# GpSimd waits, at every second group of four gathers, until all its gathers have landed

## The chip, the cores and the metric

The kernel runs on one core of a Trainium2 chip. The metric is the device time of one execution in microseconds (us). Most executions of this kernel lie within about 0.3% of each other.

## The reference, cut to what matters

`x` is 6250 x 256 in float32, with 200,000 edges `src`, `dst`, sorted by `dst`. One layer is computed:

```
xn = layernorm(x)
gnn:  h_neigh = xn @ W_neigh; keep the 32 largest of each row (h_sparse)
      summed[n] = sum over edges with dst == n of h_sparse[src];  neigh = summed / max(deg, 1)
      gnn = xn @ W_self + neigh
mix:  linear attention over all rows, a gelu/sigmoid gate, a projection
x   = x + gnn + mix
x   = x + ffn(layernorm(x))    # only the rows of the 3124 largest router weights get the ffn
```

What matters here is `summed`: for every edge a row of `h_sparse` must be fetched by its index `src` and added into the row `dst`.

## The kernel before, in words

Rows are cut into NT = 50 tiles of T = 125. A first pass (to about 275 us) computes `h_sparse` and writes it to the DRAM tensor `rows_d` as pairs of float16 (1 KB a row). Then the attention sums follow, and from about 365 us to 2216 us the main loop `positions`: ND = 5 blocks of PER = 10 positions, one position for one tile of destination rows.

Nine of ten positions in a block (s = 0 to 8) build their tile's sum from gathered rows. Edges are taken in chunks of 128, and GC = 4 chunks are a group. For each group GpSimd copies four columns of indices from `srcT` to `stage` (L573) and issues four indirect DMAs (L577), each of which fetches 128 rows of 1 KB from `rows_d` into one slot of `ring`. The ring has RING = 8 slots of a group. VectorE builds a one-hot matrix for each group (L1266), and TensorE multiplies it with the gathered rows (L916, four matmuls a group, in `visit`). The tenth position (s = 9) takes a dense tile instead: its edge counts are collected by windows in the nine positions before it (L1291 and L1293 on VectorE, L891 on TensorE), and the counts are multiplied with all of `rows_d`, which is read in three thirds into `hs` (L667, on ScalarE's DMA queue, 2.1 MB each). TensorE multiplies the thirds (L953) at s = 7, 8 and 9; `hs` holds one third, so thirds 1 and 2 are read only when the one before is used up.

The order of the gather work is set by semaphores:

- `s_land[c]`, one for each of the 32 chunks of the ring, is raised by 16 by each landed gather.
- SyncE (SP) runs a loop over all groups (L474 to L479): it waits for the four `s_land` of the group in order, and adds 1 to `s_landed`.
- TensorE waits in `visit` for `s_landed >= g + 1` (L910), and after the last matmul of a group adds 1 to `s_slot_free` (it starts at 8).
- GpSimd's queue for group g is: wait for `s_slot_free >= g + 2` (L569, that is, until group g - 7 is used up), copy the indices of group g + 1 to `stage` (L573), wait for the copy of group g's indices, issue the four gathers of group g. Groups are numbered g = 0, 1, 2, ... in what follows, q is g modulo 8.

`hold(engine, semaphore, value)` (L105) is a wait followed by a semaphore increment of a counter that nothing else waits for. GpSimd does nothing else in the main loop, and SP nothing but its counting loop.

Of the kernel before, what the change touches and what calls it, by code (L numbers as in the profile page):

```python
# [37 lines left out]
def build(nc, x_d, src_d, dst_d, w_self_d, w_neigh_d, wqkv_d, wproj_d, bproj_d, ln_g_d, ln_b_d, wg1_d, bg1_d,  # L38
# [57 lines left out]
    with ExitStack() as ctx:  # L96
# [3 lines left out]
        def sem(name):  # L100
            return ctx.enter_context(nc.semaphore(name))
# [3 lines left out]
        def hold(engine, semaphore, value):  # L105

            engine.wait_ge(semaphore, value)
            engine.sem_inc(s_alone, 1)
# [213 lines left out]
        s_landed, s_slot_free, s_stage = sem("s_landed"), sem("s_slot_free"), sem("s_stage")  # L322
# [35 lines left out]
        def tile_at(i, s):  # L358

            return i if s == PER - 1 else i * (PER - 1) + s + ND  # L360
# [13 lines left out]
        def load(engine, at, low=0, high=NG * NT + NG):  # L374
            return engine.value_load(bounds[0:1, bass.ds(at, 1)], min_val=low, max_val=high)  # L375
# [54 lines left out]
        @block.sync  # L430
        def _(sp):
            for p in range(2):
                sp.sem_inc(s_rows[p], 16)
                sp.sem_inc(s_xTout[p], 16)
            sp.wait_ge(s_const, 4)
            full = (BL - 1) * 128 * 128
            for raw, d, o in ((dst_raw, dst_d, 0), (nxt_raw, dst_d, 1), (src_raw, src_d, 0)):
                sp.dma_start(raw[:, 0:BL - 1, :],
                             d[o:o + full].rearrange("(b r e) -> r b e", r=128, e=128)).then_inc(s_edges, 16)
                sp.dma_start(raw[0:TAIL, BL - 1, :],  # L440
                             d[full + o:full + o + TAIL * 128].rearrange("(r e) -> r e", e=128)).then_inc(s_edges, 16)
                sp.dma_start(raw[TAIL:TAIL + 1, BL - 1, 0:REST - o],
                             d[full + o + TAIL * 128:E].rearrange("(a e) -> a e", a=1)).then_inc(s_edges, 16)
            for i in range(5):
                sp.dma_start(x_all[:, i * XL:(i + 1) * XL, 0:C], x_t[:, i * XL:(i + 1) * XL, :]).then_inc(s_xload[i], 16)  # L445
            sp.wait_ge(s_setup, SETUP)
            for t in (NT + 1, NT + 2):
                sp.dma_start(xT_t[:, t:t + 1, :], ctx_bd.rearrange("p k c -> p (k c)")[:, 0:KC * T].rearrange(
                    "p (a w) -> p a w", a=1)).then_inc(s_xpad, 16)
            sp.dma_start(w_neigh, w_neigh_d.rearrange("(k p) n -> p k n", p=128)).then_inc(s_wA, 16)  # L450
            sp.dma_start(wkv, wqkv_d[:, C:3 * C].rearrange("(k p) n -> p k n", p=128)).then_inc(s_wA, 16)
            sp.dma_start(wq, wqkv_d[:, 0:C].rearrange("(k p) n -> p k n", p=128)).then_inc(s_wC, 16)

            with sp.Fori(0, NT // 2) as i:
                for p in range(2):
                    sp.wait_ge(s_split, i * 2 + p + 1 + 2)
                    sp.dma_start(rows_t[:, bass.ds(i * 2 + p, 1), :], split16[:, p:p + 1, :]).then_inc(s_rows[p], 16)

            sp.wait_ge(s_gsTc, 1)
            sp.dma_start(gs_d, gsT[:]).then_inc(s_gsout, 16)  # L460
            sp.wait_ge(s_ctx, 1)
            for dst, src in ((w_self, w_self_d.rearrange("(k p) n -> p k n", p=128)),
                             (wproj, wproj_d.rearrange("(k p) n -> p k n", p=128)),
                             (bproj, bproj_d.partition_broadcast(T)),
                             (b2, b2_d.partition_broadcast(T)),
                             (wr, wr_d.rearrange("n a -> (n a)").partition_broadcast(T))):
                sp.dma_start(dst, src).then_inc(s_wF, 16)
            sp.dma_start(w1, w1_d.rearrange("(k p) n -> p k n", p=128)).then_inc(s_wB, 16)
            sp.dma_start(w2, w2_d.rearrange("(k p) n -> p k n", p=128)).then_inc(s_wB, 16)

            sp.wait_ge(s_bounds, 1)
            passes = load(sp, T_PASSES, 1, NT)
            rounds = load(sp, T_ROUNDS, 1, ROUNDS)
            with sp.Fori(0, passes) as r:  # L474
                with sp.Fori(0, rounds) as j:
                    for q in range(RING):
                        for s in range(GC):
                            sp.wait_ge(s_land[q * GC + s], (r * ROUNDS + j + 1) * 16)
                        sp.sem_inc(s_landed, 1)  # L479

            for p in range(2):
                sp.wait_ge(s_ywout[p], 16 * (NT // 2 + 1))
            sp.wait_ge(s_agg, NT)
            sp.wait_ge(s_res, NT)
            for i in range(ND):
                tile, row = tile_at(i, 0), i * PER + 3
                held = PER - 1 if i < ND - 1 else PER - 3
                sp.dma_start(yw_all[:, tile:tile + held, :], yw_t[:, row:row + held, :]).then_inc(s_ywin, 16)
                if i < ND - 1:
                    sp.dma_start(yw_all[:, i:i + 1, :], yw_t[:, row + PER - 1:row + PER, :]).then_inc(s_ywin, 16)  # L490
            for i in range(5):
                sp.wait_ge(s_fin, XL * (i + 1))
                sp.dma_start(out_t[:, i * XL:(i + 1) * XL, :], res_all[:, i * XL:(i + 1) * XL, :]).then_inc(s_out, 16)
            sp.wait_ge(s_out, 16 * 5)
# [3 lines left out]
        def _(pool):  # L498
# [65 lines left out]
            with pool.Fori(0, passes) as r:  # L564
                with pool.Fori(0, rounds) as j:
                    for q in range(RING):
                        g = (r * ROUNDS + j) * RING + q

                        hold(pool, s_slot_free, g + 2)  # L569
                        nx = (q + 1) % RING * GC  # L570
                        at = nc.s_assert_within(pool.snap(((j + start) * RING + q + 1) * GC), 0, CH,
                                                skip_runtime_bounds_check_because="start + rounds is ROUNDS at most")
                        pool.tensor_copy(stage[:, nx:nx + GC], srcT[:, bass.ds(at, GC)]).then_inc(s_stage, 1)  # L573
                        hold(pool, s_stage, g + 1)
                        for s in range(GC):
                            c = q * GC + s
                            pool.indirect_dma_start(  # L577
                                out=ring[:, c, :], out_offset=None, in_=rows_d,
                                in_offset=bass.IndirectOffsetOnAxis(ap=stage[:, c:c + 1], axis=0)).then_inc(s_land[c], 16)
# [135 lines left out]
        def _(pe):  # L715
# [191 lines left out]

            def visit(t, g, release, total):

                pe.wait_ge(s_landed, g + 1)  # L910
                slot = pe.snap((g % RING) * GC)
                visited = pe.snap(g + t)
                hot = pe.snap((visited % HOT) * GC)
                pe.wait_ge(s_oh, visited + 1)
                for s in range(GC):
                    m = pe.matmul(total, hot_slots[:, bass.ds(hot + s, 1), :], ring[:, bass.ds(slot + s, 1), :],  # L916
                                  start=False, stop=False, skip_group_check=True)
                    d = pe.matmul(deg_sum, hot_slots[:, bass.ds(hot + s, 1), :], ones16[:], start=False, stop=False,  # L918
                                  skip_group_check=True)
                d.then_inc(s_oh_free, 1)  # L920
                if release:
                    m.then_inc(s_slot_free, 1)
# [9 lines left out]
            def position(n, i, s, windows):  # L932
# [3 lines left out]
                def gathered(turn):  # L936
                    parts = window_parts(windows)
                    cuts = cut(pe, g0, g1, len(parts))
                    for at, (first, end) in enumerate(zip(cuts, cuts[1:])):
                        with pe.If(end > first):  # L940
                            with pe.Fori(first, end) as g:
                                visit(finals, g, True, total)
                        if turn and at == 0:
                            turn_x3(n + 1)
                        if at < len(parts):
                            count_window(i, *parts[at])
                    visit(finals, g1, False, total)
# [559 lines left out]
```

## Time and profile before

| what | us |
|---|---|
| median of 3 runs | 2328.24 |
| lowest, highest | 2323.92, 2329.83 |
| the profiled execution's own time | 2329.25 |
| its span, first to last instruction | 2327.5 |
| TensorE (PE) busy | 1647.6 (71%) |
| VectorE (DVE) busy | 1302.3 (56%) |
| GpSimd (POOL) busy | 1246.2 (54%) |
| ScalarE (ACT) busy | 438.3 (19%) |

The profile is of one execution. An idle time in it stands with the instruction before which the engine was idle, and with what ended that idle time; "issue" means that nothing the profile shows was waited for. POOL's busy time in the line of a gather is the writing of its descriptors, not the moving of the data. SP's counting shows only as the releaser "SPq L479". The mean granted clock of TensorE is 0.839 of its full 2.4 GHz.

### The profile page before, as it was taken

What the parts mean: (1) busy time and instruction counts of PE and PEld (TensorE: products, weight loads), DVE (VectorE), ACT (ScalarE), POOL (GpSimd) and SP (SyncE); (2) the same over time, 40 slices, a digit from 0 to 9 for tenths busy, and PEclk for the clock granted to TensorE, in tenths of its full rate; (3) what the DMA queues carried; (4) which work ended last, traced back from release to release, by engine and by line L of the source; (5) the groups of instructions that cost most, each with busy time, mean ns of one, the idle gap of its engine ahead of it and who ended that gap; (6) DMA issues with size and microseconds to landing.
All of it is one profiled execution on the core that took longest, in us unless ns stands there. A gap on an engine that the chain in (4) does not pass through costs nothing.

```text
span 2327.5 us, 44035 instructions
## 1 busy us (share of the span) xinstructions
PE 1647.6 (71%) x8607; PEld 1133.6 (49%) x8608; DVE 1302.3 (56%) x4234; ACT 438.3 (19%) x974; POOL 1246.2 (54%) x1552
## 2 busy tenths in 40 slices
PE   2498257878786677888766888757888578887640
PEld 0254154444454555555554565545556456555430
DVE  5699947666663326666324666424666226664253
ACT  0254130111111111112102221102122112221110
POOL 1155554567787755777663666553566426554000
PEclk7699678778887788999887989888899788999775
DMA  4222142233335442333442333442233433333323
GB/s 132 73 82 72 42 121 59 83 88 108 108 106 152 141 123 80 97 113 108 122 138 83 103 96 104 118 139 80 78 98 110 131 88 96 88 87 113 84 105 110
DMA packets 149254, 236.45 MB, mean 102 GB/s; under 512 B 24682, under 2 KB 113734, under 8 KB 149094
## 3 DMA queue, kind: packets, MB, share of 16 engines
q0 software_dynamic: 52480, 142.82, 21.8%
q10 hardware_dynamic: 63461, 59.79, 8.5%
q1 hardware_dynamic: 33153, 31.95, 4.3%
q8 instruction: 71, 1.16, 0.2%
q14 instruction: 89, 0.73, 0.1%
HBM read 208.46 MB, written 26.01 MB: 101 GB/s over the span
## 4 chain that ended last, share of the span: by engine, by line
PE 30%; DMA 21%; issue 16%; DVE 14%; DVEq 10%; POOL 4%; SPq 3%; ACT 0%; POOLq 0%; ACTq 0%
DMA region_k<-rows_d 18%; PE bank L916 11%; POOL ring L577 4%; PE bank L953 3%; PE bank L891 3%; PE bank L871 2%; PE bank L864 2%; DVE region_k L1293 2%; DVEq L1291 2%; DVE region_k L1291 2%; DVEq L1266 2%; DVEq L375 1%; SPq L490 1%; DVE region_r L1161 1%; SPq L445 1%
## 5 line engine op out<-in xcount | busy, mean ns | idle before, releaser
L577 POOL DMA_INDIRECT ring<-rows_d,stage x1088 | 1077.7, 991 | 321.4 <-issue 258.6
L916 PE MATMUL bank<-ring,region_v 128*125 x1260 | 447.7, 465 | 88.7 <-SPq L479 30.8
L1266 DVE SCALAR_TENSOR_TENSOR region_v<-iota,tile_start,dstT 128x500 f16 x315 | 233.7, 742 | 209.5 <-issue 187.2
L891 PE MATMUL bank<-region_k 128*125 x622 | 245.2, 479 | 129.3 <-DVE region_k L1293 94.9
L916 PEld LDWEIGHTS bank<-ring,region_v 128*125 x1260 | 194.4, 154 | 264.9 <-issue 197.3
L573 POOL COPY stage<-srcT 128x4 int32 x272 | 62.1, 228 | 408.7 <-PE bank L916 407.1
L1293 DVE TENSOR_SCALAR region_k<-iota,win_start,region_k 128x500 f16 x622 | 273.4, 440 | 2.5 <-issue 1.5
L1291 DVE TENSOR_SCALAR region_k<-iota,region_k 128x125 f16 x622 | 171.1, 275 | 137.8 <-issue 111.9
L891 PEld LDWEIGHTS bank<-region_k 128*125 x622 | 90.6, 146 | 270.9 <-issue 238.0
L918 PE MATMUL bank<-ones,region_v 128*125 128x2 f16 x1260 | 221.4, 176 | 0.0
L953 PE MATMUL bank<-region_k 125*125 125x512 f16 x250 | 85.2, 515 | 184.0 <-DMA region_k<-rows_d 184.0
L871 PE MATMUL bank<-region_v 128*125 128x256 f32 x848 | 201.5, 392 | 14.8 <-issue 14.8
L918 PEld LDWEIGHTS bank<-ones,region_v 128*125 x1260 | 198.9, 158 | 0.1
L864 PEld LDWEIGHTS bank<-region_v 128*128 128x128 f32 x1664 | 195.8, 194 | 2.8
L864 PE MATMUL bank<-region_v 128*128 128x125 f32 x1664 | 196.0, 277 | 0.0
L871 PEld LDWEIGHTS bank<-region_v 128*125 128x125 f32 x848 | 159.1, 193 | 47.1 <-issue 23.8
L953 PEld LDWEIGHTS bank<-region_k 125*125 125x125 f16 x250 | 45.6, 189 | 219.6 <-DMA region_k<-rows_d 186.7
L1344 DVE TENSOR_SCALAR col_deg<-bank 125x1 f32<-125x1 f32 x50 | 7.9, 158 | 252.3 <-PE bank L991 252.3
L661 ACT ACT_TABLE_LOAD x51 | 65.4, 1283 | 411.5 <-issue 315.6
L1336 DVE TENSOR_TENSOR region_k<-region_k,region_v 125x256 f32<-125x256 f32 x50 | 21.2, 423 | 210.4 <-DMA region_k<-in_x_dram 210.4
L695 ACT ACTIVATE region_k<-bank 125x500 f16<-125x500 f32 (+1 forms) x65 | 37.6, 578 | 499.5 <-PE bank L905 499.5
L661 ACT ACTIVATE region_v<-bank,b 128x125 f32<-128x125 f32 x416 | 111.8, 380 | 92.4 <-PE bank L864 70.2
(286 smaller groups left out, 2095.0 us busy)
## 6 DMA issues: line engine op xcount, KB each, us to landing
region_k<-rows_d ACTq DMA_DIRECT2D x10, 2125.0 KB
ring<-rows_d,stage POOLq DMA_INDIRECT x1088, 2.8
region_k<-rows_d ACTq DMA_DIRECT2D x5, 2000.0 KB
region_v<-xT_d ACTq DMA_DIRECT2D x53, 125.0 KB, 5.2
xT_d<-region_r ACTq DMA_DIRECT2D x51, 125.0 KB, 2.2
region_v<-in_x_dram SPq DMA_DIRECT2D x5, 1250.0 KB
rows_d<-region_r SPq DMA_DIRECT2D x50, 125.0 KB
region_k<-in_x_dram ACTq DMA_DIRECT2D x50, 125.0 KB
```

Source lines behind the costliest of these rows:

```text
L573: pool.tensor_copy(stage[:, nx:nx + GC], srcT[:, bass.ds(at, GC)]).then_inc(s_stage, 1)
L577: pool.indirect_dma_start(out=ring[:, c, :], out_offset=None, in_=rows_d, in_offset=bass.IndirectOffsetOnAxis(ap=stage[:, c:c + 1], axis=0 ...
L661: last = act.activation(hidT[:, n, :], bank[(7, 4)[n // 4]][:, n % 4 * T:(n % 4 + 1) * T], ACT.Gelu_apprx_tanh, bias=b1[:, n:n + 1])
L864: m = pe.matmul(bank[(7, 4)[n // 4]][:, n % 4 * T:(n % 4 + 1) * T], w1[:, k, n * 128:(n + 1) * 128], x3T[:, k, :], start=(k == 0), stop=(k ...
L871: m = pe.matmul(out, hidT[:, n, :], w2[:, n, :], start=(n == 0), stop=(n == NH - 1))
L891: m = pe.matmul(out, lo_hot[:, bass.ds(slot + u, 1), :], key_hot[:, bass.ds(slot + u, 1), :], start=False, stop=False, skip_group_check=True)
L916: m = pe.matmul(total, hot_slots[:, bass.ds(hot + s, 1), :], ring[:, bass.ds(slot + s, 1), :], start=False, stop=False, skip_group_check=True)
L918: d = pe.matmul(deg_sum, hot_slots[:, bass.ds(hot + s, 1), :], ones16[:], start=False, stop=False, skip_group_check=True)
L953: m = pe.matmul(dense_sum, counts16[:, b, :], hs[:, b - first, :], start=False, stop=False, skip_group_check=True)
L1266: dve.scalar_tensor_tensor(out=hot_slots[:, bass.ds(hot, GC), :], in0=iota[:, 0:T].rearrange("p (a t) -> p a t", a=1).to_broadcast([128, G ...
L1291: dve.tensor_scalar(lo_hot[:, bass.ds(slot + u, 1), :].rearrange("p a t -> p (a t)"), iota[:, 0:T], src_lo[:, bass.ds(at + u, 1)], None, A ...
L1293: last = dve.tensor_scalar(key_hot[:, bass.ds(slot + u, 1), :].rearrange("p a t -> p (a t)"), iota[:, 0:KEYS], win_flat[:, bass.ds(w, 1)], ...
```

## The change

Three edits. SP adds 1 to `s_landed` once before its loop, so the semaphore stands at the number of landed groups plus one. TensorE's wait is raised by one to match. GpSimd, at every odd q, waits in addition for `s_landed >= g + 1`, which with the offset means that groups 0 to g - 1, all that it has issued so far, have landed. The wait stands behind the one for a free slot and ahead of the index copy.

```diff
@@ SP, before the counting loop
             sp.wait_ge(s_bounds, 1)
+            sp.sem_inc(s_landed, 1)
             passes = load(sp, T_PASSES, 1, NT)
@@ GpSimd, in the loop over q
                         hold(pool, s_slot_free, g + 2)
+                        if q % 2:
+                            hold(pool, s_landed, g + 1)
                         nx = (q + 1) % RING * GC
@@ TensorE, visit
-                pe.wait_ge(s_landed, g + 1)
+                pe.wait_ge(s_landed, g + 2)
```

## Rows read from the trace of the kernel before

**Rows 1.** The page's groups by line: busy, mean ns, idle before.
```profile
L577 POOL DMA_INDIRECT ring<-rows_d,stage x1088 | 1077.7, 991 | 321.4 <-issue 258.6
L916 PE MATMUL bank<-ring,region_v 128*125 x1260 | 447.7, 465 | 88.7 <-SPq L479 30.8
...
L573 POOL COPY stage<-srcT 128x4 int32 x272 | 62.1, 228 | 408.7 <-PE bank L916 407.1
```

**Rows 2.** One line's view, L577: from issue to landing.
```profile
DMA to landing us min/median/max: 2.7/2.8/12.2
```

**Rows 3.** Groups by line, POOL, stretches from 500, 779, 880, 1259, 1601, 1922.
```profile
L573 POOL COPY stage<-srcT 128x4 int32 x53 | 11.5, 217 | 0.3
...
L573 POOL COPY stage<-srcT 128x4 int32 x14 | 2.8, 197 | 6.7 <-PE bank L916 6.6
...
L573 POOL COPY stage<-srcT 128x4 int32 x40 | 10.2, 255 | 35.6 <-PE bank L916 35.4
...
L573 POOL COPY stage<-srcT 128x4 int32 x33 | 7.9, 238 | 50.0 <-PE bank L916 49.9
...
L573 POOL COPY stage<-srcT 128x4 int32 x41 | 8.4, 204 | 97.1 <-PE bank L916 97.0
...
L573 POOL COPY stage<-srcT 128x4 int32 x32 | 6.8, 213 | 91.0 <-PE bank L916 91.0
```

**Rows 4.** Waits of PE, 500:779 and 779:880: total us, times, longest.
```profile
PE bank L916 <- SPq L479: 20.6, 8, 5.3
...
PE bank L916 <- SPq L479: 8.1, 2, 5.7
```

**Rows 5.** The chain of waits around 603 us: start, us, what.
```profile
603.42 3.13 DMA ring<-rows_d,stage
...
606.62 0.03 SPq L479
...
606.78 0.42 PE bank L916
```

**Rows 6.** Timeline, POOL: start, us, instruction, idle before it.
```profile
603.42 1.30 POOL L577 DMA_INDIRECT ring<-rows_d,stage  x1 [0.30 <-issue]
...
817.42 0.18 POOL L573 COPY stage<-srcT 128x4 int32 x1 [6.61 <-PE bank L916]
818.20 1.15 POOL L577 DMA_INDIRECT ring<-rows_d,stage  x1 [0.59 <-POOL stage L573]
...
823.46 0.97 POOL L577 DMA_INDIRECT ring<-rows_d,stage  x1 [0.16 <-POOL stage L573]
```

**Rows 7.** Timeline, PE: the matmul whose end frees the slot.
```profile
816.75 0.41 PE L916 MATMUL bank<-ring,region_v 128*125 x1
```

**Rows 8.** The chain: a gather's landing and three reads of thirds.
```profile
720.38 6.44 DMA ring<-rows_d,stage
...
779.21 30.77 DMA region_k<-rows_d
...
2142.01 28.59 DMA region_k<-rows_d
...
2182.45 20.34 DMA region_k<-rows_d
```

**Rows 9.** Timeline: a group's last gather, and its first matmul, twice.
```profile
1134.61 0.95 POOL L577 DMA_INDIRECT ring<-rows_d,stage  x1 [0.31 <-issue]
...
1159.07 0.43 PE L916 MATMUL bank<-ring,region_v 128*125 x1 [0.55 <-issue]
...
1475.45 0.95 POOL L577 DMA_INDIRECT ring<-rows_d,stage  x1 [0.30 <-issue]
...
1505.71 0.41 PE L916 MATMUL bank<-ring,region_v 128*125 x1
```

**Rows 10.** Timeline, POOL: copies after a long slot wait.
```profile
880.86 0.34 POOL L573 COPY stage<-srcT 128x4 int32 x1 [22.04 <-PE bank L916]
...
1259.53 0.24 POOL L573 COPY stage<-srcT 128x4 int32 x1 [28.69 <-PE bank L916]
```

## The prediction

> **What bounds the kernel now.** The groups by line come first [rows 1]: the gathers keep POOL busy for 1077.7 us, and POOL is idle for 407.1 us in front of its index copy because no ring slot is free; TensorE, on the other side of the ring, waited for landed gathers (SPq L479) only 30.8 us. So over the whole span POOL runs ahead of TensorE. That is a mean, and the same lines cut into stretches say something else [rows 3]. From 500 to 779 us POOL issued 53 groups with 0.3 us of idle time before all its copies: it never waited for a slot, and it set the pace. From 880 to 1109 us it issued 40 groups with 35.4 us of waiting, from 1259 to 1459 us 33 groups with 49.9 us, then 41 groups with 97.0 us and 32 with 91.0 us: later tiles have fewer edges, and POOL has more and more time to spare. The waits of TensorE agree: 20.6 of the 30.8 us lie between 500 and 779 us, 8.1 us between 779 and 880 us [rows 4]. In the first block (to 880 us) any time added to POOL is therefore paid, in the second it is nearly so, and in the last two it has cover.
>
> **The price of one added wait.** SP's increment and TensorE's raised bound are one semaphore instruction and a constant; nothing is late by them, and I cost them at nothing (SP does nothing else there, and TensorE's wait is the same instruction as before). The wait itself is passed when the last gather of group g - 1 is counted. Today the copy of the next group starts as that gather's issue ends. The chain shows a gather issued at 603.42 us whose landing comes 3.13 us later; its issue took 1.30 us [rows 5, 6], so 1.83 us pass between the end of the issue and the landing. (The median gather: 2.8 us [rows 2] less an issue of 0.95 us [rows 9], 1.85 us.) SP's count ends 0.10 us after the landing (603.42 + 3.13 to 606.62 + 0.03) [rows 5]. From a release to the start of POOL's copy the nearest row is the slot wait: the releasing matmul ends at 817.16 us [rows 7], the copy starts at 817.42 us [rows 6], about 0.2 to 0.26 us; I take 0.2. And after a copy that had to wait POOL is idle for 0.59 us before the first gather, after one that had not for 0.16 us [rows 6]: the register work for the gather is then no longer done ahead. That is 0.43 us more, and I take 0.45. Sum: 1.85 + 0.1 + 0.2 + 0.45 = 2.6 us a wait. Lower end 2.15 (the register work hidden after all), upper end 3.0 (0.2 us more of reaction, and now and then a late landing: the latest comes 12.2 us after its issue [rows 2]).
>
> While a third of `rows_d` is being read, a gather lands later: 6.44 us from the start of an issue of 0.95 us [rows 8, 9], that is 5.5 us after the issue's end in place of 1.85 us, 3.65 us more. I take 3.3 us, since not every group meets a read at its full rate: such a wait costs 5.9 us. One pair of groups then takes 10.3 + 5.9 = 16 us, and a read of 31 us [rows 8] holds two such waits.
>
> Queued behind the wait on POOL are the copy and all later gathers, and for these only TensorE waits. SP has nothing behind its count. There are 136 waits (half of 272 groups [rows 1]), so POOL gains about 136 x 2.15 us of standing still plus 15 reads with up to two waits each at 3.3 us more, about 360 us in all, against 407 us of slot waits that it has now. The sum has to be made by stretch.
>
> **The sum, with groups counted by their copies.** POOL's last slot wait before the tight part ends at about 500 us, where the stretch with 0.3 us of idle time begins [rows 3]. (a) From there to 779 us: the waits at groups 27 to 77, 26 of them, x 2.6 = 68 us, two of them under the read of 720 us, + 7: 74 us. Nothing covers them: TensorE catches up with POOL in this stretch already today [rows 4]. (b) 779 to 880 us: four waits up to group 85, two of them under a read: 2 x 5.9 + 2 x 2.6 = 17 us, less the 6.6 us slot wait [rows 3]: 10 us. (c) 880 us to group 137, the last that the second read of block 2 waits for: 23 waits x 2.6 + 2 x 3.3 = 66 us. Cover: the slot waits behind the first one, 35.4 - 22.0 = 13.4 us (the first, 22.0 us long [rows 10], ends where this stretch starts and is no cover), and the lead of group 137: its last gather is issued by 1135.56 us and lands some 5 us later, TensorE takes it at 1159.07 us [rows 9], 18.5 us. 66 - 13 - 19 = 34 us. (d) From the end of block 2 to 1259 us: POOL stands waiting again, no cost. (e) 1259 us to group 186: 17 waits x 2.6 + 2 x 3.3 = 51 us; slot waits behind the first of 28.7 us [rows 10]: 21.2 us; lead of group 186: issued by 1476.40 us, landed by about 1482, used at 1505.71 us [rows 9], 23.5 us. 51 - 21 - 24 = 6 us. (f) Blocks 4 and 5: 20 waits in 41 groups cost 52 us plus some 20 us for the reads, against 97.0 us; 16 waits in 32 groups 42 us against 91.0 us [rows 3]. Covered.
>
> 74 + 10 + 34 + 6 = 124 us. Two things take something back: fewer gathers run beside the reads that TensorE waits for (one with six groups beside it takes 30.77 us, one with two 28.59 us [rows 8], so about 2 us for each of the two or three reads that carry fewer), and VectorE runs ahead with its one-hots while TensorE stands still. I take 7 us off: 117 us. The sum is made against the profiled execution's own 2329.25 us: 2446 us; that lies 1.0 us above the median of the runs shown, so 2445 us.
>
> With a price of 2.15 us (a) to (e) give 62 + 9 + 24 + 0 = 95 us, less 8, 2416 us; with 3.0 us they give 85 + 12 + 43 + 13 = 153 us, 2482 us.
>
> **A rule against the change.** The Trainium skill (DMA: Bandwidth & Descriptors, Rules for kernel authors) says to issue a DMA early and to wait on its semaphore late, so that the fixed cost overlaps; it puts that fixed cost at about 2.0 us (same page, Anatomy of one DMA). By it the wait added here uncovers the fixed cost each time, and with 2.0 us in place of my 2.6 us my stretches would give some 85 us.
>
> **Rivals.** (1) *Covered everywhere.* 360 us of new standing still is less than the 407 us of slot waits [rows 1]; were the ring deep enough to carry slack from one stretch to the next, the time would stay at 2328 us. Against it: 0.3 us of slack in 279 us [rows 3], and the ring holds seven groups, some 36 us of POOL's work. (2) *Faster: the reads of the thirds get the engines.* These reads stand in the chain that ended last [rows 8], and the one with no gathers beside it took 20.34 us, with two groups still 28.59 us [rows 8]. If the pauses hand half of that 8 us to each of the 15 reads, that is -60 us; the change is faster if this exceeds what (a) to (e) cost, so it needs nearly all waits in block 1 to be free as well: 2269 us. Against it: six groups beside a read or two hardly change it (30.77 and 28.59 us). The Trainium skill (DMA: Bandwidth & Descriptors, Issuing engines are not separate DMA queues) says that transfers of all issuers interleave on the same 16 engines, which speaks for this rival. (3) *Partly covered.* TensorE and VectorE make up after each wait what they lost; only the stretch from 700 us on, where TensorE waits today, pays: 7 waits, 18 + 7 us, and (b) 10 us: some 2365 us. (4) *Dearer.* If a wait costs 4 us in the mean, because the small loads of x and xT make landings late outside the reads too (the median of 2.8 us speaks against it, the maximum of 12.2 us for it [rows 2]), then (a) 111, (b) 16, (c) 66, (e) 30: 223 us less 7, 2545 us. (5) *The wait does not do what it says*, because SP's count is ahead of POOL: excluded by the offset, which asks for all g groups issued before.
>
> **How the numbers follow.** The forecast (POOL's pace is paid for in blocks 1 and 2) has 0.80, rival 3 0.07, rival 4 0.07, rival 2 0.03, rival 1 with rival 5 0.03. The range is that of the price ends, widened towards rivals 3 and 4: 2400 to 2490 us. Faster by over 0.3% (7 us, what a measurement here can tell): 0.03; within: 0.03; slower: 0.94.
>
> **What would show it.** In the profile after, the copy on POOL has a new releaser, SPq of the counting line, some 136 times and about 360 us with about 2.2 us each outside the reads; slot waits fall from 407 to about 140 us. TensorE's idle time before L916 by SPq grows from 30.8 to about 150 us, nearly all before 1160 us. A main loop that is longer by 84 us at the end of block 1 and by 118 at that of block 2, and no longer after 1510 us than then, shows the sum right. The forecast is wrong if POOL's standing still shows under 1.8 us a wait, if blocks 4 and 5 grow, or if the reads of the thirds take under 27 us.

## The result, and the profile after

The changed kernel takes 2413.77 us (median, 2412.99 to 2414.62) against 2326.32 us before in the same comparison: a ratio of 1.0375, interval 1.0357 to 1.0393, 87 us more. Forecast were 117 us more and 2445 us. The profiled execution takes 2412.99 us, its span is 2411.2 us.

The page's groups of the changed kernel (columns as before; the gathers are L580 now, the copy L576, the matmul L919, SP's count L480), answering to [rows 1]:

```profile
L580 POOL DMA_INDIRECT ring<-rows_d,stage x1088 | 1065.5, 979 | 353.8 <-issue 269.8
L919 PE MATMUL bank<-ring,region_v 128*125 x1260 | 479.3, 490 | 223.5 <-SPq L480 166.9
...
L576 POOL COPY stage<-srcT 128x4 int32 x272 | 60.5, 222 | 481.0 <-SPq L480 385.6
```

TensorE's waiting for landed gathers rose from 30.8 to 166.9 us. POOL's idle time in front of its copies rose only from 408.7 to 481.0 us: 385.6 us of it are the new wait, and the waits of POOL (total us, times, longest) show what that replaced, the waiting for a slot, 407.1 us before:

```profile
POOL stage L576 <- SPq L480: 385.6, 124, 30.8
...
POOL stage L576 <- PE bank L919: 94.2, 20, 19.4
```

One added wait, in the tight stretch. Timeline of POOL (start, us, instruction, idle before it), and the chain of waits through the same point:

```profile
644.75 0.94 POOL L580 DMA_INDIRECT ring<-rows_d,stage  x1 [0.30 <-issue]
647.81 0.19 POOL L576 COPY stage<-srcT 128x4 int32 x1 [2.11 <-SPq L480]
648.60 0.97 POOL L580 DMA_INDIRECT ring<-rows_d,stage  x1 [0.60 <-POOL stage L576]
```
```profile
644.75 2.70 DMA ring<-rows_d,stage
...
647.53 0.03 SPq L480
647.56 0.02 issue
647.58 0.02 POOLq L108
647.60 0.06 issue
647.66 0.06 POOLq L576
647.72 0.09 issue
647.81 0.20 POOL stage L576
648.00 0.59 issue
```

The landing comes 1.76 us after the issue's end, SP's count 0.11 us later, the copy 0.25 us after that, and the first gather has 0.60 us of idle time before it where one behind an unhindered copy has 0.16 us. 2.11 + 0.44 = 2.55 us; 2.6 us was forecast. The chain shows what stands in the pause: the landing, semaphore instructions of SP and POOL, and the register instruction of the copy (POOLq L576), which begins only when the wait is over. The last 0.59 us it calls "issue"; that this is the gather's register work, no longer done ahead, is my reading of it.

By stretch (groups by line on POOL, columns as in [rows 3]; the stretches are 500 to 842, 842 to 949, 949 to 1250 and 1690 to 2240 us; they begin where 500, 779, 880 and 1601 us lie before):

```profile
L580 POOL DMA_INDIRECT ring<-rows_d,stage x209 | 204.1, 976 | 67.5 <-issue 52.4 <-POOL stage L576 14.2 <-PE bank L919 0.9
L576 POOL COPY stage<-srcT 128x4 int32 x52 | 11.2, 216 | 59.8 <-SPq L480 59.7
...
L576 POOL COPY stage<-srcT 128x4 int32 x14 | 2.7, 192 | 22.3 <-SPq L480 22.2
...
L576 POOL COPY stage<-srcT 128x4 int32 x45 | 10.9, 243 | 64.2 <-SPq L480 54.8 <-PE bank L919 9.3
...
L576 POOL COPY stage<-srcT 128x4 int32 x72 | 15.4, 214 | 160.6 <-SPq L480 91.7 <-PE bank L919 68.8
```

In the tight stretch 0.3 us of idle time before the copies became 59.8 us; in blocks 4 and 5 (the last row) 91.7 us of new waits stand where slot waits fell from 188.0 us [rows 3] to 68.8 us, and nothing is late. TensorE's waits for landed gathers, 500 to 842 us, 1350 to 1690 us (block 3) and 1690 to 2240 us:

```profile
PE bank L919 <- SPq L480: 80.2, 19, 9.9
...
PE bank L919 <- SPq L480: 22.9, 8, 8.4
...
PE bank L919 <- SPq L480: 1.2, 3, 0.4
```

The third read of each block places the loss. The chain before (start, us; blocks 1 to 4, block 5's is in [rows 8]), then after (blocks 1 to 5):

```profile
827.89 30.70 DMA region_k<-rows_d
...
1206.39 30.14 DMA region_k<-rows_d
...
1549.68 28.70 DMA region_k<-rows_d
...
1872.09 27.16 DMA region_k<-rows_d
```
```profile
900.52 25.18 DMA region_k<-rows_d
...
1300.95 24.82 DMA region_k<-rows_d
...
1642.82 26.24 DMA region_k<-rows_d
...
1958.80 25.36 DMA region_k<-rows_d
...
2266.39 20.47 DMA region_k<-rows_d
```

The starts are later by 73, 95, 93, 87 and 84 us: the loss is made in blocks 1 and 2, stays in block 3, and shrinks afterwards. And the reads themselves are shorter by 5.5, 5.3, 2.5 and 1.8 us; only the last, which has no gathers beside it, takes what it took.

### The profile page after: what moved, and what is told of

It reads as the page before. It is cut to its first block, busy times and chain, and to the rows that moved or that the text cites. A ratio compares the mean times of both kernels' runs of the same rounds, so it can differ in the third digit from the quotient of the medians.

```text
span 2411.2 us, 44172 instructions
## 1 busy us (share of the span) xinstructions
PE 1685.9 (70%) x8607; PEld 1157.9 (48%) x8608; DVE 1298.1 (54%) x4234; ACT 438.9 (18%) x974; POOL 1232.7 (51%) x1552
## 4 chain that ended last, share of the span: by engine, by line
PE 24%; DMA 22%; issue 18%; POOL 12%; DVE 11%; DVEq 7%; SPq 3%; POOLq 0%; ACT 0%; ACTq 0%
DMA region_k<-rows_d 12%; POOL ring L580 11%; PE bank L919 8%; DMA ring<-rows_d,stage 7%; PE bank L894 3%; PE bank L956 3%; PE bank L874 2%; PE bank L867 2%; DVE region_k L1296 1%; SPq L491 1%; DVEq L1294 1%; SPq L445 1%; DMA region_v<-in_x_dram 1%; DVE region_r L1164 1%; DVE region_k L1294 1%
## 5 line engine op out<-in xcount | busy, mean ns | idle before, releaser
L580 POOL DMA_INDIRECT ring<-rows_d,stage x1088 | 1065.5, 979 | 353.8 <-issue 269.8
L919 PE MATMUL bank<-ring,region_v 128*125 x1260 | 479.3, 490 | 223.5 <-SPq L480 166.9
L919 PEld LDWEIGHTS bank<-ring,region_v 128*125 x1260 | 203.9, 162 | 409.8 <-issue 349.5
L576 POOL COPY stage<-srcT 128x4 int32 x272 | 60.5, 222 | 481.0 <-SPq L480 385.6
L921 PE MATMUL bank<-ones,region_v 128*125 128x2 f16 x1260 | 226.8, 180 | 0.0
L874 PE MATMUL bank<-region_v 128*125 128x256 f32 x848 | 212.0, 406 | 10.8 <-issue 10.8
L921 PEld LDWEIGHTS bank<-ones,region_v 128*125 x1260 | 209.4, 166 | 0.0
L874 PEld LDWEIGHTS bank<-region_v 128*125 128x125 f32 x848 | 167.2, 203 | 45.7 <-issue 19.4
```

The source lines that it names most:

```text
L580: pool.indirect_dma_start(out=ring[:, c, :], out_offset=None, in_=rows_d, in_offset=bass.IndirectOffsetOnAxis(ap=stage[:, c:c + 1], axis=0 ...
L874: m = pe.matmul(out, hidT[:, n, :], w2[:, n, :], start=(n == 0), stop=(n == NH - 1))
```

## The experiments

Theory A throughout: an added wait makes POOL late by about 2.6 us, and this reaches the end only where POOL's pace, not TensorE's, sets the time; beside it the waits shorten the reads of the thirds. Ratios are to the kernel before, on the same chip. The diffs are against the changed kernel unless another is named, and are cut to the lines that matter.

**The offset without the wait.**

```diff
                         hold(pool, s_slot_free, g + 2)
-                        if q % 2:
-                            hold(pool, s_landed, g + 1)
```


> The offset of the landed count and TensorE's raised bound stay, GpSimd's added wait is left out. Theory A (the time is GpSimd's standing still in front of its copy, where its pace is TensorE's): as before, 2326 us, within 7 us; no idle time of POOL by SPq, some 407 us by slots. Rival B (TensorE or SP pay for the changed count): up to 2414 us.

Measured: 2323.68 us, ratio 0.9997 (0.9985 to 1.0009). SP's increment and TensorE's bound cost nothing. Rival B is out.

**The wait, asking for one group less.**

```diff
                         if q % 2:
-                            hold(pool, s_landed, g + 1)
+                            hold(pool, s_landed, g)
```


> The wait stays at every odd group, but asks for one landed group less (all but the group issued last). That group's predecessor landed some 3 us before the issue ends, so the wait is passed at once. Theory A: 2326 us, at most 10 us more from waits under the reads of the thirds; idle time of POOL by SPq under 40 us. Rival C (the cost is the instructions of the wait and the register work behind it, not the landing): the 0.45 us of register work at 66 exposed waits, 2350 us or more.

Measured: 2321.76 us, ratio 0.9988 (0.9978 to 0.9998). POOL's copies in this kernel, groups by line (L472 is SP's raise of the count, L480 its loop):

```profile
L576 POOL COPY stage<-srcT 128x4 int32 x272 | 59.8, 220 | 412.3 <-PE bank L919 355.4 <-SPq L472 29.4 <-SPq L480 25.9
```

The same instructions in the same places are free once they wait for a landing that is over; rival C is out. The price is that of the youngest group's landing and what is queued behind it. The two SPq terms are 55.3 us, where under 40 us were expected; 29.4 us of them are one wait at the very start, told below.

**The wait at every group.**

```diff
-                        if q % 2:
-                            hold(pool, s_landed, g + 1)
+                        hold(pool, s_landed, g + 1)
```


> The wait at every group instead of every odd one. Theory A: a group now takes 5.2 + 2.6 = 7.8 us of POOL; POOL's chain for 272 groups needs some 2120 us from 287 us on and bounds the whole main loop: a queue model made from the trace of before gives 390 to 410 us more, 2720 us; slot waits nearly gone (under 40 us). Rival D (the cost is one of the positions' starts or of fewer gathers beside each other, roughly in proportion to the number of waits): twice the 87 us, 2500 us.

Measured: 2772.4 us, ratio 1.1929 (1.1909 to 1.1949): 448 us for twice the waits that cost 87 us, so not in proportion (rival D). The waits of this kernel:

```profile
POOL stage L575 <- SPq L480: 786.1, 271, 9.4
PE bank L918 <- SPq L480: 568.6, 107, 9.6
...
PE bank L955 <- DMA region_k<-rows_d: 12.4, 5, 3.7
```

No slot wait is left: POOL bounds the whole main loop, and TensorE waits 12.4 us for the reads in place of 184. The queue model's 390 to 410 us were too low by a tenth: the mean wait is 786.1 / 271 = 2.9 us, above the 2.1 us of one that meets no read.

**The waits in blocks 1 and 2 alone.** GpSimd's loop is cut in two, each with the old body:

```diff
-                with pool.Fori(0, rounds) as j:
+                with pool.Fori(0, 18) as j:      # with the wait at odd q
...
+                with pool.Fori(18, rounds) as j: # without it
```


> The waits stand only in the first 18 of 34 rounds (groups 0 to 143, blocks 1 and 2); GpSimd's loop is split in two for that. Theory A: all of the cost lies there, 2410 to 2420 us; since the later waits made the reads of the thirds shorter and took back some 6 us in blocks 4 and 5, this kernel is a few us slower than the changed one (2417 us). Rival E (each wait costs the same wherever it is): 18/34 of 87 us, 2372 us.

Measured: 2423.8 us, ratio 1.0435 (1.0416 to 1.0455), above the changed kernel's 1.0375. All of the cost lies in the first 18 rounds; the later waits gave some 14 us back (0.6%). Rival E is out.

**The waits from round 18 on alone.** The same cut, with the wait in the second loop only.

> The waits stand only from round 18 of 34 on (groups from 144, the end of block 2 to block 5). Theory A: POOL has slot waits to spare there, so nothing is late, and the reads of the thirds end 2 to 4 us sooner as with the changed kernel: 2324 - 10 = 2314 us, faster than both kernels; reads of 25 to 29 us in place of 27 to 30. Rival E (a wait costs the same everywhere): 16/34 of 87 us more, 2365 us. Rival G (the shorter reads come from TensorE being late, not from the pauses): 2324 us, reads as before.

Measured: 2314.27 us, ratio 0.9951 (0.9937 to 0.9964): 11 us faster than before, as forecast from the last run. It beats both kernels. Its copies (L576 in rounds 0 to 17, L593 from 18 on), and the third reads of blocks 2 to 4 in its chain:

```profile
L576 POOL COPY stage<-srcT 128x4 int32 x144 | 34.2, 237 | 121.6 <-PE bank L936 120.4 <-issue 0.5
L593 POOL COPY stage<-srcT 128x4 int32 x128 | 26.4, 206 | 274.2 <-SPq L480 180.7 <-PE bank L936 93.1
```
```profile
1203.28 26.54 DMA region_k<-rows_d
...
1545.16 25.68 DMA region_k<-rows_d
...
1861.25 25.82 DMA region_k<-rows_d
```

180.7 us of waits cost nothing here, and the reads are 3.6, 3.0 and 1.3 us shorter than before though TensorE is not late. Rival G is out: the shorter reads come from the pauses.

**The wait behind the copy.**

```diff
                         hold(pool, s_slot_free, g + 2)
-                        if q % 2:
-                            hold(pool, s_landed, g + 1)
...
                         pool.tensor_copy(stage[:, nx:nx + GC], ...).then_inc(s_stage, 1)
+                        if q % 2:
+                            hold(pool, s_landed, g + 1)
                         hold(pool, s_stage, g + 1)
```


> At odd groups the wait for the landed count stands behind the index copy instead of ahead of it, before the gathers. The landing is waited for just as long. If the price of 2.55 us has 0.45 us of register work that can't be done ahead and 0.2 us of copy in it, the copy is now hidden: 0.35 us less a wait at some 40 paid waits, 2400 us (14 us less than the changed kernel). If the register work too is hidden by the earlier copy: 2.15 us less 0.2, 2390 us. If only the landing counts: 2414 us.

Measured: 2406.21 us, ratio 1.0344 (1.0328 to 1.036), 7 us less than the changed kernel. Timeline of POOL:

```profile
643.43 0.21 POOL L574 COPY stage<-srcT 128x4 int32 x1
646.23 0.97 POOL L580 DMA_INDIRECT ring<-rows_d,stage  x1 [2.58 <-SPq L480]
```

From the end of the gather before (643.43) to the next gather are 2.80 us, against 3.06 + 0.79 - 0.94 = 2.91 us in the timeline of the changed kernel (645.69 to 648.60). Only 0.1 us a wait is saved in the trace (7 us over some 40 paid waits would be 0.2 us), where 0.35 us were expected: most of what follows the release still stands behind it.

**Every eighth group.**

```diff
-                        if q % 2:
+                        if q == RING - 1:
                             hold(pool, s_landed, g + 1)
```


> The wait only at every eighth group (q = 7), 34 waits in place of 136. Theory A: 7 waits in the tight stretch of block 1 and one at group 79 are paid, 2.6 us each, one or two under a read at 5.9: some 20 us; block 2's lead (18 us at group 137) covers its six waits; reads a little shorter, 2 to 5 us back: 2340 us (2332 to 2348). Rival D (in proportion to the number of waits): 22 us, 2346 us, so not told apart by the time alone but by the place: A puts all of it before 880 us.

Measured: 2331.11 us, ratio 1.003 (1.002 to 1.0039), 7 us, just under the range expected: a quarter of the waits cost a twelfth. The starts of the reads are later by 17 us at the second read of block 1, by 12 us at the first read of block 2, by 7 us at its third and by 1 us at the last of all: the loss is in block 1, as theory A has it, and what takes nearly all of it back is more than the 2 to 5 us that I gave to shorter reads. From issue to first matmul the 14 reads after the first take 391.1 us, against 408.5 us before and 404.0 us in the run with the offset alone.

**A pause in place of the wait.** The kernel before, with work on GpSimd that waits for nothing:

```diff
                         hold(pool, s_slot_free, g + 2)
+                        if q % 2:
+                            for n in range(22):
+                                pool.memset(idle[:, n * 12:(n + 1) * 12], 0.0)
```


> The kernel before with 22 small fills of a scratch tile on GpSimd at every odd group, between its slot wait and its copy: about 2 us of standing still for the gathers, with nothing waited for. Theory A (what counts is that POOL comes later): near the changed kernel, scaled by 2.0 to 2.6 us: 2326 + 60 to 75 us = 2385 to 2400 us, all of it in blocks 1 and 2. Rival F (the landing itself counts, that no gathers are in flight): 2326 to 2340 us. For the reads of the thirds: if the pace of the gathers makes them shorter, they are shorter here too (25 to 29 us); if it takes an empty queue, they stay as before.

Measured: 2362.16 us, ratio 1.0155 (1.014 to 1.0171), between the two ranges expected. The pause turned out half as long as meant (timeline of POOL):

```profile
643.36 1.03 POOL L573 MEMSET idle<- 128x12 f16 x22
644.32 0.20 POOL L577 COPY stage<-srcT 128x4 int32 x1
```

1.03 us each, 30 pauses up to group 85: 31 us, and the third read of block 1 starts 29 us later. With 1.0 in place of 2.6 us block 2 should lose nothing (23 - 13 - 19 < 0), and its third read is 29 us late too. So lateness by itself costs what theory A says; rival F is out. 6 us more in blocks 3 and 4 stay unexplained. The reads are hardly shorter (29.4, 29.1, 32.2, 31.1, 29.3 us from issue to first matmul in blocks 1 and 2): a pause of 1 us does little.

**Every fourth group, from round 18 on.** `q % 4 == 3` in the second loop.

> As the run with the waits from round 18 on, but only at every fourth group (q = 3 and 7). A read of a third then meets one wait in place of two. If each wait under a read takes its share of what made the reads shorter (24 us over 14 reads with two waits), the reads are 1 to 2 us shorter than before and the time is 2319 us, between 2325 (before) and 2314 (waits at every second group).

Measured: 2319.3 us, ratio 0.9961 (0.9947 to 0.9976). From issue to first matmul the nine reads from block 2's last to block 5's second take 255.5 us, against 263.1 us before and 246.4 us with the wait at every second group: half the waits, 45% of the gain in the reads. The time can't tell such shares: the intervals of the two ratios overlap.

**The same places, a pause in place of the wait.**

```diff
-                        if q % 4 == 3:
-                            hold(pool, s_landed, g + 1)
+                        if q % 4 == 3:
+                            for n in range(110):
+                                pool.memset(idle[:, n * 2:(n + 1) * 2], 0.0)
```


> As the run before this one, but at q = 3 and 7 from round 18 on GpSimd runs 110 small fills of a scratch tile (some 5 us, as long as a wait under a read) and waits for nothing. Theory P (the reads are shorter because fewer gathers come in that time): reads as short as with the wait at the same places, within 1 us. Rival Q (it takes a queue that has run empty, which the wait makes sure of): reads as before, 27 to 30 us. The total may be up to 20 us longer, because the pause is 5 us outside the reads too, where the wait is 2.5 us.

Measured: 2329.81 us, ratio 1.0005 (0.9996 to 1.0015). The pauses, groups by line (32 of them, 3.35 us each):

```profile
L591 POOL MEMSET idle<- 128x2 f16 x3520 | 107.3, 113 | 62.7 <-PE bank L938 62.2 <-issue 0.5
```

The nine reads take 261.0 us: 2 us less than before, where the wait gives 7.5 us. That is not clear of noise: the run with the offset alone, whose gathers are never held up, has 260.8 us, and the execution profiled here was the slowest of ten (2338.69 us).

Packets that started in the first 20 us of a read tell more finely. On ScalarE's queue, which carries the read, there are 1320 to 1430 before (mean 1378), 1353 to 1570 with the pause (1488), 1380 to 1654 with the wait (1540); the offset alone has a mean of 1411. Of the gathers' packets there are 679 before, 674 with the offset alone, 584 with the pause and 527 with the wait in the mean. So a pause without a landing does thin out the gathers beside a read, by less than the wait; it was also shorter than a wait under a read (3.35 against 5 to 6 us), and 95 to 152 packets is about that proportion, which speaks for theory P. For the length of the reads neither theory P nor rival Q is settled by this.

**From round 16 on.** The cut at 16 in place of 18.

> The waits at every odd group from round 16 on in place of round 18 (from group 128, so that they meet the two reads of block 2 that TensorE waits for last). Lead of group 137 before: 18.7 us; the five waits to it cost 3 x 2.6 + 2 x 5.9 = 20 us, the read before them ends 3 us sooner: 0 to 2 us late, and the next read is 4 us shorter. 2312 us (2309 to 2315) against 2314 us with round 18.

Measured: 2318.12 us against 2328.6 us before in that comparison, ratio 0.9954 (0.9938 to 0.9969). That is the same as with round 18 (0.9951); the intervals are some 3.5 us wide to each side, so the 2 us that I expected could not have shown.

## Why the prediction was right, and where its sizes were off

**What bounds the kernel: right.** Block 1 has no slack in POOL, block 2 too little, the rest enough. Early waits alone cost more than all waits (1.0435), late waits alone cost nothing. Rival 1, that 407 us of slot waits cover the 360 us, would have needed slack to move from the late blocks to the early ones.

**The price of a wait: right.** 2.55 us against 2.6 us. The waits stand for 385.6 us in all where 360 us were forecast (136 x 2.15 us are 292 us, and two dear waits in each of 15 reads would add 99 us, so the 360 us were an estimate between). 30.8 us of the 385.6 us is one wait that I had not seen. I wrote that SP does nothing but count, but its loop begins only at 325 us, after it has issued its weight loads, and group 1 waited for that:

```profile
293.22 1.10 POOL L580 DMA_INDIRECT ring<-rows_d,stage  x1 [0.30 <-issue]
325.07 0.66 POOL L576 COPY stage<-srcT 128x4 int32 x1 [30.75 <-SPq L480]
```

TensorE takes group 1 only at 365 us, so it cost nothing. Slot waits fell to 94.2 us, further than the 140 us forecast.

**(a), 500 to 779 us: 74 us forecast, 67 us found.** From the copy of group 27 to the end of group 78's gathers POOL took 274.3 us before and 341.3 us after. Idle time before the copies is 59.8 us in place of 0.3 us; the other 7 us are the first gathers' longer gaps, less 4 us that the gathers' issues got shorter (994 to 976 ns in this stretch, some 210 of them). Only one of the two waits that I put under the read of 720 us was dearer. In 10 of the 14 reads that have gathers beside them only one wait is longer than 4 us.

**(b), to the end of block 1: 84 us with (a) forecast, 73 us found at the third read's start, 68 us at its last matmul.** The two reads took 26.8 and 25.2 us in place of 30.8 and 30.7 us.

**(c), block 2: 34 us forecast, 22 us found** (73 to 95 us at the third reads). One of the 23 waits, at group 93, stands behind the slot wait that opens the stretch and was free. **(e), block 3: 6 us forecast, none found**, though TensorE came to wait 22.9 us for gathers there. **(f), blocks 4 and 5: nothing forecast, 9 us given back** (93 to 84 us; 84 us is the difference of the two profiled executions, 87 us that of the medians).

The term that was mis-sized is the shortening of the reads. I gave it 2 us for each of two or three reads, from one read with six groups beside it and one with two [rows 8]. It came in most of them: the 14 reads after the first take 384.7 us from issue to first matmul in place of 408.5 us, and without the one of block 2 that TensorE came late to, 346.3 in place of 376.5 us, 30 us less (a few us of this are noise: the run with the offset alone has 404.0 us where the kernel before has 408.5 us). Of the 37 us between the 124 us of the sum and the 87 us measured, this would be most, if each us of a read is a us of the time; the runs show that for the late blocks alone (11 us in the run from round 18 on, some 14 us against the run with the early waits). One sign that I had named of a wrong forecast did come: reads under 27 us. Six of the 13 reads with gathers beside them are (24.9 to 26.8 us), and none was before. The sign of the price (under 1.8 us a wait) and that of the late blocks (longer) did not.

The packets in the traces show what changed beside the reads. In the first 20 us of a read the gathers had 673 to 728 packets before and 417 to 499 after (the second read of block 5: 528 and 455). ScalarE's queue had 1320 to 1440 and 1569 to 1668, and the sum of the two stayed near 2070 (1885 to 2133 before, 2028 to 2123 after). So in that time the read got what the gathers did not take. Over the whole read, some have fewer gathers beside them (17, 16, 16 before and 14, 14, 16 after in block 3) and some as many (9 and 9 at the second read of block 5, 28.6 and 26.7 us; 13 and 13 at the first, 28.5 and 29.0 us).

My comparison of 30.77 with 28.59 us compared two reads with 690 and 528 packets of gathers in their first 20 us, where the pauses bring these to between 417 and 499; it was no measure of what a pause does. Rival 2 was thus the right mechanism at half the size that I tried on it (2 of 4 us a read), beside the forecast and not in its place. That a rule of the Trainium skill speaks for it (DMA: Bandwidth & Descriptors, Issuing engines are not separate DMA queues: all issuers' transfers interleave on the same engines) is borne out: reads of 25 to 30 us with waiting gathers, 27 to 32 us with unhindered ones, 20.5 us with none.

The lead terms held. In block 2 the 13.4 us of slot waits that I counted as cover were used up (of the 9.3 us left 9.0 us are the first slot wait, which had been 22.0 us), and at groups 137 and 186 no lead was left: TensorE waited 6.0 and 3.8 us for them. My upper sum (2482 us) does not take off the few us for shorter reads that the other two do.

## What to carry to other kernels

The mean slack of a producer says little: cut its idle time by stretch, and count a wait only where the stretch has none. A wait for the youngest transfer costs its landing (1.8 us here) and the register work that can't run ahead of it (0.4 us), while a wait for the transfer before it is free. Where a producer has time to spare, the same wait can pay, because fewer gathers then run beside a large read that someone else waits for; put it there alone (0.9951 against 1.0375).

## What the runs showed that was not expected

- Nine of the 12 reads of 2.1 MB that have gathers beside them and that TensorE stood waiting for got 1.6 to 5.5 us shorter when the gathers beside them were issued in pairs of groups with a landing between. The packet counts point to the slower pace of the gathers. Whether an empty queue adds to it stays open: a pause of 3.35 us in place of a wait of 5 to 6 us gave 2 us over nine reads, which is within noise, and the wait 7.5 us.
- A fill of a few columns on GpSimd takes 47 ns in a row of 22 (1.03 us) and 30 ns in a row of 110 (3.35 us), less than I had expected of both, so both pauses were shorter than meant.
- With TensorE waiting more, its mean granted clock fell from 0.839 to 0.819, and to 0.766 with the wait at every group. By stretch it fell from 0.85 to 0.77 in the tight one, where TensorE has 80.2 us of waits for gathers as cover, and from 0.87 to 0.84 in block 2, where TensorE was busy for 298.9 us in place of 283.9 us. The chain of the changed kernel goes through POOL's gathers from 1094 to 1258 us; but how much of block 2's 22 us is this slower clock, and how much POOL's pace, no run separates.
